# First four pairs' tokens and last four pairs' output rows by one-hot matmuls instead of DRAM, in a one-core decoder layer with a routed mixture of experts

## The reference, cut to what matters

```python
x = x + attn(layernorm(x))                   # 16 heads of 16, rotary, causal
x = x + graph_mix(ctx_512, layernorm(x))     # top 76 of 256 similarities per row, symmetrised
x = x + moe(layernorm(x))

def moe(x):                                  # x: (1024, 256)
    scores = sigmoid(x @ gate_w)             # 64 experts, 8 groups
    # the 4 best groups, in them the 6 best experts; weights scaled to a sum of 2.5
    # every expert takes its first CAP = 48 tokens, in order of the tokens
    h = silu(buf @ w_gate[e]) * (buf @ w_up[e])        # buf: (64, 48, 256), F = 96
    out = h @ w_down[e]                                # (64, 48, 256)
    y = segment_sum(out[expert, place] * weight, token)
    return y + (silu(x @ ws_gate) * (x @ ws_up)) @ ws_down   # the shared expert
```

## Time and profile before

| | us |
|---|---|
| time before, median of 3 runs | 335.44 (333.37 to 337.35) |
| the profiled execution's own time | 335.68 |
| span of its trace (first to last instruction) | 333.9 |
| TensorE busy, share of the span | 229.0, 69% |
| VectorE | 202.3, 61% |
| GpSimd | 142.1, 43% |
| ScalarE | 97.5, 29% |

### The profile page before, as it was taken

The page is one execution under the profiler, slowest core; times in us unless marked ns, Lnnn a source line. Parts: engine busy times, 40 slices in busy tenths (PEclk is TensorE's granted clock), DMA queues, the critical chain, the costliest instruction groups (busy, mean ns, idle before and its releaser), DMA issues.

```text
span 333.9 us, 5159 instructions
## 1 busy us (share of the span) xinstructions
PE 229.0 (69%) x1816; PEld 166.2 (50%) x1816; DVE 202.3 (61%) x646; ACT 97.5 (29%) x156; POOL 142.1 (43%) x185
## 2 busy tenths in 40 slices
PE   6398059279879876975365850385289999986676
PEld 2277057168567655754253630232146776654354
DVE  2127999999999999999425238441115453431464
ACT  1504621153524345354135302201002332332000
POOL 2582660546620220127604727777602455467000
PEclk9969659759999999999569655569589999998789
DMA  6501999049299997003998119950089999911796
GB/s 198 167 0 38 128 128 156 1 77 128 73 139 307 395 385 276 2 0 141 306 288 249 37 28 281 261 122 13 8 158 216 236 264 240 268 65 33 257 416 218
DMA packets 37081, 55.97 MB, mean 168 GB/s; under 512 B 6696, under 2 KB 26931, under 8 KB 37056
## 3 DMA queue, kind: packets, MB, share of 16 engines
q1 hardware_dynamic: 31680, 47.75, 55.9%
q10 hardware_dynamic: 768, 3.54, 5.0%
q0 software_dynamic: 4608, 4.36, 4.4%
HBM read 32.93 MB, written 25.69 MB: 176 GB/s over the span
## 4 chain that ended last, share of the span: by engine, by line
PE 24%; DVE 24%; issue 11%; another core or an unknown queue 8%; DMA 6%; ACT 6%; POOL 3%; SPq 1%; ACTq 0%; DVEq 0%; POOLq 0%
DVE arena L1160 5%; DVE arena L1058 4%; PE unit L648 4%; DVE arena L1053 3%; DMA arena<-expert_rows 3%; DMA arena<-slot_rows 3%; PE unit L596 3%; PE gen L570 3%; PE proj L667 3%; PE gen L588 2%; PE outp L710 1%; DVE st L1084 1%; ACT arena L803 1%; POOL expert_rows L1016 1%
## 5 line engine op out<-in xcount | busy, mean ns | idle before, releaser
L994 POOL DMA_INDIRECT slot_rows<-rows,arena x48 | 47.5, 990 | 16.7 <-issue 13.3
L1016 POOL DMA_INDIRECT expert_rows<-arena x32 | 31.1, 972 | 36.4 <-ACT arena L868 29.4
L803 ACT ACTIVATE arena<-unit 128x1024 f32<-128x1024 f32 x24 | 24.5, 1024 | 52.1 <-PE unit L492 40.6
L896 POOL TENSOR_SCALAR nmean<-mv 128x2 f32<-128x2 f32 x12 | 2.8, 234 | 85.0 <-DVE mv L1091 77.8
L492 PE MATMUL unit<-arena 128*128 128x256 bf16 (+1 forms) x128 | 30.4, 254 | 0.0
L1053 DVE MAX8 arena<-arena 128x8 f32<-128x256 f32 x80 | 30.0, 414 | 0.2
L1160 DVE TENSOR_REDUCE arena<-unit 128x4 f32<-128x1024 f32 (+1 forms) x24 | 28.9, 1212 | 0.6 <-PE unit L479 0.5
L1058 DVE MATCH_REPLACE8 arena<-arena 128x256 f32<-128x256 f32 x72 | 29.0, 410 | 0.0
L490 PE MATMUL unit<-arena 96*128 96x128 bf16 (+1 forms) x96 | 23.3, 260 | 5.9 <-ACT arena L803 5.5
L491 PE MATMUL unit<-arena,identb 128*128 128x128 bf16 x128 | 26.9, 228 | 0.0
L478 PE MATMUL unit<-arena 96*128 96x128 bf16 (+1 forms) x96 | 17.7, 269 | 12.1 <-DMA arena<-arena 11.5
(11 more groups left out here) (203 smaller groups left out, 552.8 us busy)
## 6 DMA issues: line engine op xcount, KB each, us to landing
ring<-in_w_gu SPq DMA_DIRECT2D x16, 384.0 KB
expert_rows<-blank SPq DMA_DIRECT2D x8, 768.0 KB, 9.2
arena<-in_w_gu SPq DMA_DIRECT2D x16, 384.0 KB, 11.8
arena<-expert_rows SPq DMA_DIRECT2D x7, 768.0 KB, 9.1
slot_rows<-blank SPq DMA_DIRECT2D x1, 4608.0 KB, 18.6
arena<-slot_rows ACTq DMA_DIRECT2D x12, 288.0 KB
arena<-ring_dn SPq DMA_DIRECT2D x24, 128.0 KB, 6.3
ring_dn<-in_w_dn SPq DMA_DIRECT2D x16, 192.0 KB
```

The costliest lines, as they stand in the source:

```text
L803: act_fn(prob[:, n, :], unit_at((key, b)), ACT.Exp, scale=D ** -0.5).then_inc(unit_free((key, b)), 1)
L994: pool.indirect_dma_start(out=slot_dram, out_offset=bass.IndirectOffsetOnAxis(ap=place[:, t, k:k + 1], axis=0), in_=rows[:, t, :], in_offs ...
L1016: pool.indirect_dma_start(out=z_dram, out_offset=bass.IndirectOffsetOnAxis(ap=rowi[:, p:p + 1], axis=0), in_=yrow[:, p % NY, :], in_offset ...
```

## The change

1. Head. The tokens of pairs 0 to 3 (gather group 0) no longer come through `slot_rows`. In three new steps of the list, H0 and H1 (after D1e3) and H2 (at its end), and once more after the last routing group, VectorE compares the router's goals of two tiles with the numbers of the 384 slots (`head_picks`), and TensorE multiplies x3 with these matrices of ones and zeros into `proj` (`head_tokens`: 4 matmuls with 384 columns for each two tiles, 16 in all). These pairs, now two bundles of two (`HEAD` = 2), go through gate_up, hidden and down ahead of the main loop, between `shared_in(0)` and `shared_in(1)`; their tokens are still placed too. Their metadata come by two small DMAs (`first_rows`), after all placements.
2. Both `shared_out` are ahead of the main loop; `keep_clock(30)` comes behind them and behind the head's `ht_free`; `keep_clock(18)` is gone. The three memsets go to VectorE.
3. Main loop: 15 bundles (13 of two pairs, two single); gather groups 1 to 7. The ring has 19 places; pairs 19 and 20 are loaded when the head's bundle 0 has passed `down`, 21 to 31 after the first gathers are issued.
4. Tail. The last four pairs (`NQ`) are not scattered. TensorE adds them to the residual: for each of 8 tiles one matmul of the identity with `res` and four with `hot` (ones and zeros, token by slot) into eight PSUM areas. VectorE makes the four `hot`, 1024 columns each, in the last steps of the main loop, from `count` (an iota of 1024 on GpSimd, issued between the last placement and the first scatter). The 9 pieces are now added by GpSimd (2 x 256 columns) and VectorE (4 additions of 256 columns).
5. A new order of stages: among others, one placement fewer ahead of D1e3 on GpSimd and one more between D1e3 and D23; another iota (384 numbers, `aims`) in V0; in D3a1's ring loads three pairs fewer.

```diff
-BUNDLES = [(0,), (1,)] + [(p, p + 1) for p in range(2, NP - 2, 2)] + [(NP - 2,), (NP - 1,)]
+BUNDLES = [(p, p + 1) for p in range(0, NP - 2, 2)] + [(NP - 2,), (NP - 1,)]
+HEAD = PPG // 2
+HEAD_COLS = PPG * 2 * CAP
-RP = 22
+RP = 19
# SP, after the stages
+            for p in range(HEAD):
+                refill(p)
             for k in range(KE):
                 sp.wait_ge(placed[k], 16 * NT)
+            slot_half(sp, 1, 0)
+            first_rows(sp)
+            for g in range(2, NX + 1):
                 slot_half(sp, g, 0)
+            for p in range(HEAD, NP - RP):
+                refill(p)
             for s in range(NY):
-                sp.wait_ge(scattered[s], 16 * (NP // NY))
+                sp.wait_ge(scattered[s], 16 * len(range(s, NS, NY)))
+            sp.wait_ge(y_full, NB)
# TensorE
+            def head_tokens(n):
+                if n == 0:
+                    emptied(pe, "proj", ("otok", B - 1))
+                pe.wait_ge(x3_ready, n + 1)
+                pe.wait_ge(picks_ready, n + 1)
+                for t in range(TPB * n, TPB * n + TPB):
+                    for c in range(2):
+                        last = mm(proj[:, c * 512:c * 512 + HEAD_COLS], x3[:, t, c * P:(c + 1) * P], picks[:, t, :], start=(t == 0), stop=(t == NT - 1))
             positions(NG2 - 1)
             shared_in(0)
+            head_tokens(B - 1)
+            for n in range(HEAD):
+                gate_up(n)
+            hidden(0)
+            hidden(1)
+            for n in range(HEAD):
+                down(n)
+            pe.wait_ge(hid_ready, HEAD)
             shared_in(1)
             shared_out(0)
+            shared_out(1)
+            pe.wait_ge(ht_free, HEAD)
+            pe.wait_ge(placed[KE - 3], 16 * NT)
+            keep_clock(WARM, outp)
...
+            pe.wait_ge(hot_ready, NQ)
...
             pe.wait_ge(y_free, NP)
+            for t in range(NT):
+                to = tail_area[t][:, 0:E]
+                mm(to, identf[:, :], res[:, t, :], start=True, stop=False)
+                for q in range(NQ):
+                    last = mm(to, hot[q][:, t * P:(t + 1) * P], yrow[:, (NS + q) % NY, :], start=False, stop=(q == NQ - 1))
+                last.then_inc(last_full, 1)
# ScalarE
             shared_silu(0)
+            for n in range(HEAD):
+                gate_silu(n)
             shared_silu(1)
# GpSimd
-            link(pool.memset(xgT, 0.0))
-            link(pool.memset(rowi, FAR))
-            pool.memset(wslot, 0.0).then_inc(moe_pads, 1)
             place_rows(TPB * KE)
+            pool.iota(count, pattern=[[1, T]], base=0, channel_multiplier=0, allow_small_or_imprecise_dtypes=True).then_inc(count_ready, 1)
-            for p in range(NP):
+            for p in range(NS):
                 scatter(p)
+            for i, (t, cols) in enumerate(PIECES):
+                gp.wait_ge(z_in[i % NZ], 16 * (i // NZ + 1))
+                z = zin[:, i % NZ]
+                pool.tensor_tensor(z[:, 1:3, cols], z[:, 1:3, cols], z[:, 4:6, cols], ALU.add).then_inc(rest_added, 1)
# VectorE
+            head_picks(B - 1)
...
+            for m in range(HEAD):
+                take_tokens(m)
+            for m in range(HEAD):
+                gated(m)
+            for m in range(HEAD):
+                hidden_turned(m)
             shared_hidden(1)
             shared_add(0)
+            shared_add(1)
...
+            def one_hot(q):
+                v.tensor_scalar(hot[q], count, slot_token[:, q:q + 1], None, ALU.is_equal).then_inc(hot_ready, 1)
-                half = mark(v.tensor_tensor(z[:, 0:3, cols], z[:, 0:3, cols], z[:, 3:6, cols], ALU.add))
+                half = mark(v.tensor_tensor(z[:, 0, cols], z[:, 0, cols], z[:, 3, cols], ALU.add))
+                ve.wait_ge(rest_added, i + 1)
                 need(half)
                 pair = mark(v.tensor_tensor(z[:, 0, cols], z[:, 0, cols], z[:, 1, cols], ALU.add))
-                rest = mark(v.tensor_tensor(z[:, 2, cols], z[:, 2, cols], res[:, t, cols], ALU.add))
+                ve.wait_ge(last_full, t + 1)
+                rest = mark(v.tensor_tensor(z[:, 2, cols], z[:, 2, cols], tail_area[t][:, cols], ALU.add))
```

268 lines of the change are left out of this document (154 added, 114 removed).

## The result

The changed kernel took 353.17 us (median of 4 runs, 350.72 to 355.56), the kernel before beside it 336.39 (4 runs, 333.37 to 339.24): ratio 1.053, 95% interval 1.039 to 1.067. The forecast was 331 with a range of 324.5 to 338.5. The profiled run of the changed kernel took 350.72, span 349.0 (before 333.9).

The account below looks back on a forecast made before the run. Before: GpSimd's placements, then TensorE in the main loop beside full DMA queues, then the tail's transfers. Forecast: T0 252.7 + loop 51.0 + tail 25.7 = 329.4 span, + 1.8 outside = 331.2, so 331 us; range 324.5 to 338.5.

Parts of the forecast that it names:

- the 5.4 for the three late releases: Head: three TensorE releases (head_full, gu_full, ht_full) fall into GpSimd's placements, each taken 1.8 late, 5.4 in all.
- land in 5.5, before T0: Token loads: ScalarE's gathers, issued at about 245 behind shared_silu(1), land 5.5 later, before the main loop's first transposes.
- T0: Start of the main loop's first token transposes: 247.94 in the kernel before, forecast at 252.7.
- the tail's 25.7: From the last down's end to the span's end: TensorE's 80 passes bound it, 25.7, a gain of 2.6.
- C: Rival, head: releases late by 2.9 to 5.1 each push T0 to 255.7 or 258.8, time 334.2 or 337.3; chance 0.26.
- C's milder case: Head: the three releases late by their mean of 2.9, giving T0 255.7 and time 334.2.
- the same load: Main loop's DMA: one group's gather less, one pair's weights more, each 576 KB, so weights land by about 291.
- 51.0 forecast from T0: Main loop, T0 to E: 52.9 from the first gate_up, less 3.16 for one bundle, plus 1.2 before it.
- the two metadata DMAs are small; cover: all else: Placements and gathers: the head's two metadata loads were taken as small and covered by all other work.
- E: End of the main loop's last down: 305.62 in the kernel before, forecast at 303.7.
- rival D: Tail: VectorE and GpSimd take turns, 2.4 a piece, end at E + 27.5, +1.8, time 333; chance 0.07.
- F: Rival, tail: TensorE stays at 1.2 GHz, its 80 passes take 35 to 38, +15, time 346; chance 0.05.

Follow-up runs that it names:

- e2: Changed kernel with GpSimd waiting once for the head's first gate_up between the sixth and seventh of its last twelve placements: 339.78 us, ratio 1.019.
- e3: Changed kernel without the last twelve placements, so those tokens miss their routed experts: 334.21 us, one run.
- c1: Changed kernel untouched, on a chip without "remote" waits: 320.30 us, ratio 1.011 to the kernel before.
- e1: Changed kernel with ScalarE's token loads issued ahead of shared_silu(1) and SyncE's ahead of the two refills: 342.60 us, ratio 1.026.
- e4: Changed kernel with GpSimd's additions of the tail given to VectorE: 346.89 us, ratio 1.039.
- c2: Kernel before, untouched, profiled on the same chip as c1: 318.24 us for its one run, median there 315.97 of 13 runs.
- e5: e3 with GpSimd writing its row of counts twelve more times, without transfers, on a chip without "remote" waits: 312.87 us, one run.
- e16: e5 repeated on another chip, again without "remote" waits: 313.88 us, one run.
- e14: Changed kernel with slot_meta(0) one step later, four refills ahead of the wait for placements, first_rows behind all token loads: 318.56 us, ratio 1.006.
- e15: e14 with SyncE issuing both halves of every token load and VectorE alone adding in the tail: 316.72 us, ratio 1.003.
- e7: e6 with VectorE alone adding in the tail, as in e4: 321.28 us, ratio 1.016; on another chip 321.55, 1.012.
- e6: Changed kernel with shared expert and keep_clock ahead of the head, its matmuls behind the placements, token loads issued first: 322.08 us, ratio 1.017.

## Why the prediction was wrong

Three terms failed: the 5.4 for the three late releases, and "land in 5.5, before T0", which put the wait for the token loads at nothing, and the tail's 25.7, which priced VectorE and GpSimd as if each were alone. The span was forecast at 329.4 and came at 349.0, 19.6 more: 13.7 in T0 (266.39 for 252.7), 1.5 in the loop, 4.4 in the tail.

The 13.7 of T0 divide so. H's last matmuls ended 4.4 earlier than forecast (223.48 for 227.9). From there to the end of the head's last down it took 25.8, not 12.8: 13.0 more. shared_in(1), both shared_out and keep_clock took 13.4, not 12.0: 1.4 more. And TensorE waited 3.75 for the loads.

**The late releases.** The mechanism was seen and placed right (three releases of TensorE fall into the placements); the size of the term was wrong. I bounded one release by 5.1, the largest seen, and held C back by "the delay can't outlast the placements". That sentence came nearly true, but the placements last to 240.54 and the release was due at about 230, so by the same sentence one release could cost 10. The delay isn't a price per release: e2 and e3 show that on this chip a release may be held until GpSimd stops issuing. With releases in time it takes 7.1 from H's last pass to the end of down (c1), where 7.4 was forecast, and here 25.8. The forecast had 5.4 for the late ones; they cost 18.7, and in that is the clock, which the prediction's term had left out: the head's down ran at 0.50 behind the waits and took 3.68 for 1.95. C, 0.26, named the direction, with a worst case of 258.8. (C's milder case should read 256.0, 247.3 + 3 x 2.9, not 255.7.)

**ScalarE's loads.** "ScalarE's gathers are behind its shared_silu(1), at about 245 then, and land in 5.5" was two errors. They were issued at 254.56: the silu hangs on the end of the head, as I had seen, and the head ended at 249.2, not 240.7. And they took 11.7, behind the refills of four pairs that I had let go as "the same load". SyncE's halves I had at 242.2, with the last placement; its refills, which wait for the head's first down, held them to 249.57, a path that is nowhere in the prediction. e1 measured the order of the loads by itself: against e4 on the same chip 5.3 of T0 and 2.1 of the loop. That the 11.7 come from the refills is argued from the queue rows: in c1, where two of the refills were issued 12 ahead of the loads, the same loads took 5.8.

**The main loop.** 51.0 forecast from T0, 52.5 and 51.9 measured: near by luck. I took over 52.9 from the kernel before, with the late releases of its loop in it; on a prompt chip the same stretch takes 48.4 (c2, 239.76 to 288.16). The changed kernel's loop can take 46.9 where loads and weights are there (e5, e16). What fills the rest in c1 is the wait of 3.4 for the second group and first_rows and 1.6 of slower passes behind it. On the first chip the loop began at granted clock 0.50, without a further wait for data, and had late releases. I had written that "the two metadata DMAs are small; cover: all else". They are small, 12 KB each, and land 9.1 to 10.6 after issue (c1, e14, e15) like the large ones beside them.

**The tail.** 30.1 from E for 25.7. Row loads at E + 2.4 (first chip) and E + 1.6, forecast 0.6. TensorE's matmuls, 2.16 a tile, were expected to end last and ended first. The last sum came at E + 27.7 and 28.0 against the 22.8 of my sum: rival D, to which I had given 0.07 and a price of 1.8, was the case. It costs 2.5 to 3.8 against VectorE alone (e4 against the changed kernel, e7 against e6, e15 against e14: 2.5, 3.8, 3.0 at the last sum). From the first landing to the last sum my sum had 17.6, D 19.4; it took 20.8, and the first landing was 1.7 later behind E. I had seen that the engines would be together "both under the pieces' pace", and priced each as if it were alone.

**Right:** the stages ahead of 220 (D23 within 0.4 of before, last placement 0.7 earlier), the iotas, TensorE's clock in the tail (F did not come), the head's work, and that the placements set T0 where releases are prompt.

**The account.** First chip: T0 + 18.5, loop - 5.2, tail + 1.8. Other chips, in spans: T0 + 1.4, loop - 0.7, tail + 1.6, together 2.3; the medians differ by 4.3 with an interval of 0.2 to 1.9%. Of the changed kernel's parts, the matrices at the end are worth about 3.5 and GpSimd's share of the sums costs about 3. The head frees four pairs from a loop whose start is then set by its loads and by TensorE's clock behind the wait for them.

## What to carry to other kernels

Work put under another engine's stretch is free only if its results get out and if nothing that is due at the end of the stretch queues behind it: here ScalarE's four load issues, 1.8 us of work, stood behind the whole head, and SyncE's behind two refills that waited for the head. When work is taken out of a loop, ask what the loop's first steps wait for: shorter steps want their data earlier, and a small load issued beside large ones lands with them. Count a wait of TensorE ahead of a loop twice: here the first steps behind it ran at about half the clock. And before a time is explained, run both kernels on a second chip: here the ratio was 1.053 on one and 1.011 on another, and the cause of most of the loss was in the first alone.

## What the runs showed of the hardware that was not expected

- On one chip results of TensorE were taken late ("remote") while GpSimd issued indirect DMAs, by 2 to 10 us, and once 3.3 after the last one; the kernel before took 334 to 336 there. On four other chips no trace shows such a wait, on one of them (c1, c2) with these same two kernels, and the kernel before took 316 to 317. ScalarE's result was taken within 0.1 even there (240.19 + 0.33 by VectorE at 240.55). A pause of 2.5 in GpSimd's issuing let the release out (e2). What the chips differ in, whether it is lasting, and whether a busy GpSimd without transfers would hold releases too, is open.
- Behind waits of 3.4 to 4.9 TensorE's next steps ran at a granted clock near 0.5, 16 passes in 2.8 instead of 1.52 (changed kernel, e4, c1); straight behind keep_clock, or after a wait of 1.25, at 1.00 (e1, c2).
- Beside a GpSimd addition of two 128x512 inputs, VectorE's addition of 256 numbers with both inputs in SBUF took 900 ns on the mean at one line and up to 1.49 us, alone 425; with one input in PSUM 414. GpSimd's took 1.40, VectorE's 0.95 for 768 numbers: giving GpSimd the two thirds made the whole slower.
- Two loads of 12 KB landed 9.1 to 10.6 after issue beside eight loads of 288 KB, whether issued second (c1) or last (e14, e15).
